# A gated attention and feed-forward block on one core: the last batch's attention in two halves of 112 queries, exponential loads of 128 columns, and a new order of steps

## What is computed

```python
x = x + tanh(g_xattn[0]) * _L0_xattn_ref(_layernorm(x), ctx_1024, ...)   # both inputs normalised again inside
x = x + tanh(g_ffn[0]) * _L0_ffn_ref(_layernorm(x), W1, b1, W2, b2)
# _L0_xattn_ref
Q = (q @ Wq + bq).reshape(B, Nq, H, Hd).transpose(0, 2, 1, 3)
K, V = ...  # the same from the context
attn = softmax(einsum('bhqd,bhkd->bhqk', Q, K) * SCALE)
out = einsum('bhqk,bhkd->bhqd', attn, V) ...; return out @ Wo + bo
# _L0_ffn_ref
gamma = mean(abs(W)); Wq = clip(round(W / (gamma + EPS)), -1.0, 1.0)   # for W1 and W2
h = relu(einsum('bsd,fd->bsf', x, Wq1) + b1)
out = einsum('bsf,df->bsd', h, Wq2) + b2
```

## Time and profile before

| | us |
|---|---|
| three runs | 959.28, 960.85, 962.5 |
| median | 960.85 |
| the profiled execution | 958.05 |
| its span (first to last instruction) | 956.3 |
| PE busy in the span | 879.9 (92%) |
| DVE, ACT, POOL busy | 731.7, 640.1, 294.1 |

### The profile page before, as it was taken

How to read it: one execution, slowest core, us unless ns; L and a number is a source line. 1 busy time by engine, 2 the same in 40 slices (tenths; PEclk the granted TensorE clock), 3 DMA queues, 4 the chain that set the end, 5 groups by cost and what they waited for, 6 DMA issues and landing times.

```text
span 956.3 us, 21961 instructions
## 1 busy us (share of the span) xinstructions
PE 879.9 (92%) x8708; PEld 658.2 (69%) x8708; DVE 731.7 (77%) x1370; ACT 640.1 (67%) x1330; POOL 294.1 (31%) x513
## 2 busy tenths in 40 slices
PE   2898899889999999999999999999989999788778
PEld 0454666656777678867787678966776678567647
DVE  3557899999888877798777877799778777878521
ACT  0877568866987577767767687677777666587421
POOL 1050265354323243034412353024303242114023
PEclk9898999899999999999999999999999999989979
DMA  9389825680147014340317014150422023300100
GB/s 272 125 234 224 214 62 151 156 216 1 33 98 186 1 33 97 77 121 1 86 44 181 16 33 97 42 145 1 115 46 69 1 62 86 93 1 1 37 10 23
DMA packets 51718, 83.47 MB, mean 87 GB/s; under 512 B 6329, under 2 KB 33465, under 8 KB 50617
## 3 DMA queue, kind: packets, MB, share of 16 engines
q1 hardware_dynamic: 51184, 82.05, 33.4%
q10 hardware_dynamic: 432, 0.02, 0.0%
HBM read 41.67 MB, written 3.67 MB: 47 GB/s over the span
## 4 chain that ended last, share of the span: by engine, by line
PE 71%; DVE 13%; ACT 5%; DMA 5%; issue 2%; SPq 2%; POOL 1%; ACTq 0%; DVEq 0%; POOLq 0%
PE ps_fill L519 45%; PE ps_pv L566 8%; PE ps_score L534 7%; PE ps_exp L550 6%; DVE row_max L830 4%; PE ps_fill L576 3%; DVE p_parts L838 3%; DMA h_parts<-g_f 1%; DVE ctx_t L915 1%; SPq L438 1%; PE ps_fill L624 1%; ACT p_parts L703 1%; DMA ctx_raw<-ctx_in 1%; ACT ps_exp L704 1%; DMA k_stack<-k_stage 1%
## 5 line engine op out<-in xcount | busy, mean ns | idle before, releaser
L830 DVE TENSOR_REDUCE row_max<-ps_score 128x1 f32<-128x750 f32 x256 | 239.0, 933 | 53.0 <-PE ps_score L534 50.1
L703 ACT ACTIVATE p_parts<-ps_exp 125x448 f16<-125x448 f32 x384 | 209.0, 544 | 69.2 <-PE ps_exp L550 59.6
L838 DVE TENSOR_TENSOR p_parts<-ps_exp,p_parts 125x448 f16<-125x448 f32 x384 | 230.8, 616 | 25.2 <-ACT ps_exp L704 23.8
L704 ACT ACTIVATE ps_exp<-ps_exp 125x448 f32<-125x448 f32 x384 | 211.2, 550 | 0.0
L534 PE MATMUL ps_score<-k_stack,q_stack 96*128 96x375 f16 x512 | 127.9, 331 | 16.8 <-DVE row_max L830 16.3
L550 PE MATMUL ps_exp<-q_stack,k_stack 100*125 100x224 f16 x768 | 129.7, 266 | 7.8 <-DVE p_parts L838 6.8
L519 PE MATMUL ps_fill<-ctx_t,wk_hi 128*128 128x375 f16 x512 | 122.9, 323 | 0.6 <-ACT lifted L741 0.5
L519 PE MATMUL ps_fill<-wv_hi,ctx_t 128*125 128x512 f16 x384 | 121.6, 379 | 0.5 <-ACT lifted L758 0.5
L566 PE MATMUL ps_pv<-v_now,p_parts 125*128 125x66 f16 x3072 | 115.0, 194 | 4.3 <-DVE p_parts L838 2.9
L566 PEld LDWEIGHTS ps_pv<-v_now,p_parts 125*128 125x128 f16 x3072 | 108.6, 98 | 12.9 <-issue 4.7
L550 PEld LDWEIGHTS ps_exp<-q_stack,k_stack 100*125 100x125 f16 x768 | 88.3, 137 | 33.1 <-DVE p_parts L838 12.3
(11 more groups left out here) (150 smaller groups left out, 1388.3 us busy)
## 6 DMA issues: line engine op xcount, KB each, us to landing
k_stack<-k_stage SPq DMA_DIRECT2D x96, 187.5 KB, 2.7
v_now<-v_stage SPq DMA_DIRECT2D x32, 346.5 KB
ctx_raw<-ctx_in SPq DMA_DIRECT2D x8, 1344.0 KB
h_parts<-w1t SPq DMA_DIRECT2D x16, 512.0 KB, 4.5
h_parts<-w2t SPq DMA_DIRECT2D x16, 512.0 KB, 4.9
x_for_q<-x SPq DMA_DIRECT2D x16, 256.0 KB, 3.7
q_stack<-q_stage_hi SPq DMA_DIRECT2D x64, 56.0 KB, 2.3
x_residual<-x SPq DMA_DIRECT2D x14, 256.0 KB, 3.0
```

Of the source, the lines that this page charges most:

```text
L703: nc.scalar.activation(ph[0:KR, unit, :], ps_exp[0:KR, u, 0:2 * NQ], ACT.Exp, scale=EXP_SCALE)
L704: nc.scalar.activation(ps_exp[0:KR, u, 0:2 * NQ], ps_exp[0:KR, u, 0:2 * NQ], ACT.Exp, scale=EXP_SCALE).then_inc(exp_done, 1)
L830: nc.vector.tensor_reduce(mx[:, i // 2, i % 2:i % 2 + 1], ps_score[:, :, 0:KH], AX.XY, ALU.max) \
L838: nc.vector.tensor_tensor(pl[0:KR, unit, :], ps_exp[0:KR, u, 0:2 * NQ], ph[0:KR, unit, :], ALU.subtract).then_inc(p_split, 1)
```

## The change

**The last batch's attention** is cut by queries. `score.i` now takes head i%16 for half i//16, 112 queries as stationary columns (no row is done twice). `expo.i` makes four matmuls of 112 moving columns, over pairs of heads of one half, 48 steps as before; `pv` takes a pair of heads of one half (24 matmuls, the last two of them with 112 stationary columns); `mr`, `split` and `ot` follow the halves; `divide` has one half at a time. Tile 0 of the batch (its queries 0 to 95, beside 32 rows of batch 6) needs the first half alone, so `op.0` now stands before the last `pv`; and `op`, statistics, `rstd2`, `norm2`, `yt`, `f1`, `f2`, the biases and the stores go tile by tile: an `f1` step is four chunks of one tile (32 matmuls of 128 columns).

**In all batches** `expo` loads 128 columns of `k_stack` where it loaded 125, but for the last of the six key blocks. The three extra columns are the next block's keys; their exponentials land in three partitions that nobody reads. Blocks still begin at 125 x kt.

**All three tables** are new. The diff, cut to its core:

```diff
@@ -42,135 +42,139 @@
 OPENING = """
-    load.0@0 stat.6@0 norm.6@0 w_hi.0@0 stat.7@0 bias_sum.0@0 norm.0@0 w_hi.1@0 norm.1@0 cx.0@0 w_hi.2@0 xx.0@0
...
+    stat.6@0 load.0@0 w_hi.0@0 bias_sum.0@0 f2.3@0 stat.7@0 stat.0@0 stat.1@0 stat.2@0 w_hi.1@0 w_hi.2@0 norm.0@0
...
-    split.0@0 kq.3@0 vc.2@0 part.44@-1 split.1@0 ctx.0@2 pv.15@-1 take.13@-1 xx_lo.1@1 f2_add.3@-2 part.45@-1
...
+    xb.0@39 vc.0@36 score.10@0 split.2@0 max.8@0 take.15@-1 k.0@1 part.0@0 expo.3@0 store.0@18 vc.1@36 max.9@0
...
+        LAST = B - 1
+        HQ = NQ // 2
+        LAST_AT = LAST * NQ - tiles_before(LAST) * P
...
                     copy_kq(i, n)
                 elif kind == "vc":
                     copy_v(i, n)
+                elif kind == "store" and n == LAST:
+                    sp.wait_ge(out_ready, tiles_before(n) * 2 + 2 * i + 2)
+                    j = tiles_before(n) + i
+                    sp.dma_start(out.rearrange("b q d -> (b q) d")[j * P:(j + 1) * P, :], xb[:, i, :]) \
+                        .then_inc(out_stored, 16)
                 elif kind == "store":
                     sp.wait_ge(out_ready, tiles_before(n + 1) * 2)
                     for i in range(tiles_of(n)):
@@ -523,18 +554,17 @@
 
             def score(i, n):
 
-                h, t = i // 2, i % 2
+                h, t = (i % H, i // H) if n == LAST else (i // 2, i % 2)
                 if t == 0 and h % 4 == 0:
                     pe.wait_ge(kq_landed[h // 4], n * 96 + 96)
                 if n == 0 and i == 0:
                     pe.wait_ge(bias_row_ready, 3)
                 else:
                     pe.wait_ge(max_taken, n * 32 + i)
-                for half in range(2):
-                    last = pe.matmul(ps_score[:, half, 0:KH],
-                                     q_stack[0:SPLIT_ROWS, h, QSTART[t]:QSTART[t] + P],
-                                     k_stack[0:SPLIT_ROWS, h, half * KH:half * KH + KH],
-                                     start=True, stop=True)
+                q = half(t) if n == LAST else slice(QSTART[t], QSTART[t] + P)
+                for s in range(2):
+                    last = pe.matmul(ps_score[0:q.stop - q.start, s, 0:KH], q_stack[0:SPLIT_ROWS, h, q],
+                                     k_stack[0:SPLIT_ROWS, h, s * KH:s * KH + KH], start=True, stop=True)
                 last.then_inc(scores_ready, 1)
 
             def expo(i, n):
@@ -546,19 +576,42 @@
                     pe.wait_ge(shift_rows, n * 8 + (h // 2 + 1))
                 if n * 48 + i >= 3:
                     pe.wait_ge(p_split, n * 48 + (i - 2))
-                for kt in (2 * u, 2 * u + 1):
-                    last = pe.matmul(ps_exp[0:KR, u, (kt % 2) * NQ:(kt % 2) * NQ + NQ],
-                                     k_stack[0:STACK_ROWS, h, kt * KR:kt * KR + KR],
-                                     q_stack[0:STACK_ROWS, h, :], start=True, stop=True)
+                if n == LAST:
+                    for c in range(4 * u, 4 * u + 4):
+                        hc, kt = 2 * (h % 8) + c // KT, c % KT
+                        rows = P if kt < KT - 1 else KR
+                        last = pe.matmul(ps_exp[0:rows, u, (c % 4) * HQ:(c % 4 + 1) * HQ],
+                                         k_stack[0:STACK_ROWS, hc, kt * KR:kt * KR + rows],
+                                         q_stack[0:STACK_ROWS, hc, half(h // 8)], start=True, stop=True)
+                else:
+                    for kt in (2 * u, 2 * u + 1):
+                        rows = P if kt < KT - 1 else KR
+                        last = pe.matmul(ps_exp[0:rows, u, (kt % 2) * NQ:(kt % 2) * NQ + NQ],
+                                         k_stack[0:STACK_ROWS, h, kt * KR:kt * KR + rows],
+                                         q_stack[0:STACK_ROWS, h, :], start=True, stop=True)
                 last.then_inc(logits_ready, 1)
 
+                if n == LAST:
+                    for c in range(2 * KT):
+                        w = P if c < 2 * KT - 1 else HQ
+                        for part in (ph, pl):
+                            last = pe.matmul(
+                                ps_pv[0:w, c // KT * 2 * VW:(c // KT + 1) * 2 * VW],
+                                part_of(part, 3 * (h % 2) * 2 * NQ + c * HQ, w),
+                                v_now[0:KR, c % KT, 2 * (h % 8) + c // KT].rearrange("p a b -> p (a b)"),
+                                start=(c % KT == 0 and part is ph), stop=(c % KT == KT - 1 and part is pl))
+                    last.then_inc(pv_done, 1)
+                    return
...
+                        if n == LAST:
+                            m = 4 * (i % 4) + 2 * t
+                            last = pe.matmul(ps_fill[SPLIT_ROWS:STACK_ROWS, bank, half(t)],
+                                             mhl[0:HQ, i // 4, m:m + 2, :], ident16[0:HQ, 0:HQ],
+                                             start=True, stop=True, tile_position=(0, SPLIT_ROWS))
+                            continue
...
+                    if n == LAST:
+                        if i % 4 == 0:
+                            pe.wait_ge(y_split, tiles_before(n) + i // 4 + 1)
+                        for j in range(4):
+                            m = slice((i % 4 * 4 + j) * P, (i % 4 * 4 + j + 1) * P)
+                            last = three(ps_fill[:, bank, j * P:(j + 1) * P], lambda a, c: w1q[:, c, m],
+                                         lambda a, c: o_t[a][:, n % 2, c, tile(i // 4)], order=((0, 0), (0, 1)))
+                        last.then_inc(fill_ready, 1)
+                        return
...
+                    if n == LAST:
+                        m = 4 * (i % 4)
+                        nc.scalar.activation(q_stack[SPLIT_ROWS:STACK_ROWS, m:m + 4, half(i // 4)]
+                                             .rearrange("p (j h) n -> p j h n", j=2),
+                                             ps_fill[SPLIT_ROWS:STACK_ROWS, bank, 0:NQ]
+                                             .rearrange("p (j n) -> p j n", j=2).unsqueeze(2)
+                                             .to_broadcast([4, 2, 2, HQ]), ACT.Copy).then_inc(shift_rows, 1)
+                        return
...
             def score(i, n):
 
                 dve.wait_ge(scores_ready, n * 32 + (i + 1))
+                if n == LAST:
+                    h, t = i % H, i // H
+                    if i % 4 == 0:
+                        dve.wait_ge(max_split, (n - 1) * 8 + (h // 2 + 2))
+                    nc.vector.tensor_reduce(mx[0:HQ, h, t:t + 1], ps_score[0:HQ, :, 0:KH], AX.XY, ALU.max) \
+                        .then_inc(max_taken, 1)
+                    return
...
+                if n == LAST:
+                    m = 2 * (h % 8)
+                    nc.vector.tensor_reduce(o_sum[0:HQ, h // 8, m:m + 2, :],
+                                            ps_pv[0:HQ, 0:4 * VW].rearrange("p (h s d) -> p h d s", h=2, s=2),
+                                            AX.X, ALU.add).then_inc(o_taken, 1)
+                    return
...
+                    if n == LAST:
+                        stats_tile(i, n)
+                    elif i == tiles_of(n) - 1:
...
                     variance_prep(dve, nc.vector, n)
                     rstd_refine(dve, nc.vector, r1, rstd1_step, n * 8 + 2, mv1[:, :, 0], norm1_ready)
                 elif kind == "rstd2" and n == B - 1:
-                    variance_finish(dve, nc.vector, n)
-                    rstd_refine(dve, nc.vector, r2[:, :, 0:tiles_of(n)], rstd2_step, n * 7 + 1, mv2[:, 0:tiles_of(n), 0],
-                                    norm2_ready)
+                    variance_finish(dve, nc.vector, n, i)
+                    rstd_refine(dve, nc.vector, r2[:, :, i:i + 1], rstd2_step, (n + i) * 7 + 1, mv2[:, i:i + 1, 0],
+                                norm2_ready)
...
```

370 lines of the change are left out of this document (227 added, 143 removed).

## The result

| six runs each, on the same chips | median us | lowest to highest |
|---|---|---|
| before | 957.68 | 955.4 to 962.5 |
| changed | 946.51 | 941.63 to 950.62 |

The ratio is 0.9859, with a 95% interval of 0.9826 to 0.9891: the change makes the kernel 1.4% faster. The prediction was 949.5, with 944 to 955 as the range of its likeliest case; the profiled execution took 946.35, its span 944.6, where the sum had 945.0. As a sum that is right to 0.4 us. Its terms are not, and the experiments are about them. The median was forecast 3.0 too high for a reason of its own: 2.8 us were added to the sum, by which the first three runs of the kernel before lie above its profiled execution (958.05).

What follows compares the result with a forecast made beforehand. PE paces the middle batches and idles at the ends. 956.3 - 7.8 - 3.0 - 2.0 + 1.5 = 945.0 span; 1.75 outside it and 2.8 for the median give 949.5, likeliest case 944 to 955, full range 936 to 963.

Steps and rivals of the forecast that it cites:

- The tail: From the end of the last batch's first `op.0` to the end: 43.7 us left, 7.8 us less than before.
- (a): Tail: PE waits 1.9 us before the last `pv`, as `op_add` and statistics stand ahead of `part` on DVE.
- (b): Tail: PE waits 1.8 us before `yt.0` for tile 0's row statistics and norm.
- (e): Tail: PE waits 0.6 to 0.7 us before `yt.1`, whose statistics chain of 4.1 us runs under `f2.0`.
- 34.1 us of matmuls at full clock: Tail: the matmul time left for PE behind the last batch's `op.0`, 34.1 us.
- The start: ACT's opening: three `w_hi` before the norms and the context's norm first; 2.0 us less, from 0 to 3.
- Rival B: Start and last attention: new orders also shrink PE's idle 22.3 and 12.7 us, by 11.7, to 937.8; chance 0.22.
- 128 columns: Exponentials, batches 0 to 6: faster loads behind short matmuls, 0.43 us a batch, 3.0 us less, between 0 and 4.6.
- the 91.6: Length in us taken for a middle batch of the kernel before, expected to become 91.2.
- Narrow matmuls: Last batch: 192 matmuls of 112 columns leave some slower loads showing; 1.5 us more, from 0 to 3.6.
- SP's queue: Middle and last rounds: context and `kq.3` copies land just in time under DVE's work; costed at nothing.
- rival D: Context lands late in four rounds, DVE and PE wait; 7 us a round at most, 967 at 4.4; chance 0.10.

Runs made afterwards that it cites:

- experiment 10: Changed kernel with ACT's old order at the very start, and `w_lo.0` behind the row statistics on DVE: 947.32 us, ratio 0.9883.
- experiment 1: The changed kernel run again with no edit, also called the repeat: 945.75 us, ratio 0.9861 against the kernel before.
- experiments 7 and 8: Changed kernel with SP's queue in the old order from batch 2: 940.59 us; with the engines' old order in the rounds too: 943.65 us.
- experiment 6: Changed kernel with the last `kq` group ahead of the store in SP's queue, in rounds 2 to 6: 954.48 us, ratio 0.9973.

## Why the prediction was right, and where its steps failed

- **The tail, forecast -7.8, measured -4.85.** Mechanism right, size off. The waits came as worked out: (a) 1.8 for 1.9, (b) 1.9 for 1.8, (e) 1.1 for 0.6 to 0.7. The idle time of the tail is 8.9 us for the 9.6 of the sum. What failed is the term 34.1 us of matmuls at full clock: PE was busy for 37.7. Behind the pauses (a) and (b), 3.6 us of idle time in 5.7 (2.5 to 3.7 in the eleven profiles), it was in every run at the lower level for 6.8 us, here busy for 5.99 of them, and half of that, 3 us, is lost. The prediction had named this as a possible loss of up to 2.4 us and not taken it, though the earlier trace rows already showed such a drop behind the pause of 5.4. The cut was also reached at the lower clock (`op.0` 4.20 us for 2.7).
- **The start, forecast -2.0, measured -8.4 to batch 2** (about -8 over all profiles, 0.7 of it work that moved behind the point; 0.9 was forecast for loads). The first turn came at 24.98 for the forecast 25.2, but mostly by another cause (experiment 10). In this pair the first score comes at 69.9 for 74.4 and batch 2 at 283.0 for 291.4; over all profiles 3.0 of the 8 us are there at the first score (70.3 for 73.3) and 7.8 at the first exponentials of batch 1 (183.8 for 191.6), so the larger part lies in batch 0's attention. Rival B foresaw a gain of this kind without naming a wait. Its cause stays open: no single wait is as large, and up to 5.8 us can be the clock (experiment 1).
- **128 columns, forecast -3.0.** 0.2 to 0.3 us a batch in the old order, 0.5 to 0.8 in one batch of the new one, for the 0.43 of the step. In the five rounds of the changed kernel PE is busy for 1.9 us less than before for the same work, near the 2.1 forecast, but it is idle for 7.1 us instead of 5.7, and 0.5 is left. The time does not resolve it alone. In one point the text was wrong: batches 2 to 4 last 108.6 to 108.7 us in the kernel before, batch 5 97.3 and batch 6 103.8; no row gives the 91.6.
- **Narrow matmuls, forecast +1.5, measured +1.35 in that stretch, but that is a balance of larger parts.** PE is idle there for 10.0 us in place of 13.4 and busy for 4.8 more; 3.7 of that is the clock, as PE is busy at the lower level for 13.0 us in place of 5.6, and 1.1 is matmul time. In it, 192 matmuls at 51 ns for 46.7 are 0.8 us, and the 32 loads of 112 columns at most 0.5. The match with the forecast is luck. Matmuls of 128 columns cost nothing more: in the first layer of the changed kernel those of 128 columns start 50 to 60 ns apart (timeline of PE):

```profile
930.74 0.22 PE L550 MATMUL ps_fill<-o_t_hi,w_ternary 128*128 128x128 f16 x1
...
930.79 0.22 PE L550 MATMUL ps_fill<-o_t_lo,w_ternary 128*128 128x128 f16 x1
...
930.85 0.22 PE L550 MATMUL ps_fill<-o_t_hi,w_ternary 128*128 128x128 f16 x1
```

  The rule of the Trainium skill (TensorE: Matmul & The Clock Gate, Back-to-back issue gap), 81 ns for sustained matmuls of this width, does not hold here; the measurement decides.
- **SP's queue, forecast 0, measured a cost of 3 to 6 us** (experiments 7 and 8). The timing of the context was right to 0.1 us at its issue, and rival D showed itself as soon as the context was pushed by 2 us (experiment 6). What failed is the step's list of who waits: it had the readers of the copies' targets, not the writers of their source.
- The sum came out by luck: for the same work the opening's unforeseen 4.8 us paid for the tail's 3 and the rounds' 1.6.

## What to carry to other kernels

For every transfer that is moved in a queue, ask two questions: who reads what it writes, and who must wait to overwrite what it reads. An order of engines and an order of a DMA queue have to be tested apart as well as together; here the faster engine order hid most of the price of a slower queue, and taking the queue back gave another 3 to 6 us. And where a pause at the end is cut in pieces, the clock can still fall behind the pieces: count the matmuls behind them at the lower level until a trace shows otherwise. Where two orders are compared between two points of one engine, see first which steps each has ahead of the point; and set idle time, busy time and time at the lower level side by side, since a stretch can match a forecast while its parts do not.

## What the runs showed of the hardware

- In the changed kernel a load of 125 or 112 stationary columns in fp16 has a mean of 135 to 152 ns in the records, one of 128 columns in fp16 or fp8 has 97 to 112, at any starting column seen here. Under a stream of 112-column matmuls the slow kind gives 58 ns a matmul and the fast kind 51, so the recorded length of a load says little on what it costs.
- PE's clock fell to half in stretches of 3.4, 6.8, 10.2 and once 13.7 us. Some came at the same place of the program in every run (4.7 to 5.8 us behind the cut), others moved (17.0 and 3.4 us of them before batch 2 in two profiles of one kernel), and 10.2 us of them ahead of batch 0's first exponentials did not make the repeat later there than the changed kernel's first profile (92.3 and 92.0 us).
- With the old order of the engines, a wait of 7.05 us for DMA copies in DVE's queue became one of 7.05 us on PE in the same round: with one score buffer nothing lies between them.
